# Value products of two pairs of heads in four column groups in the full attention of a twelve-sublayer decoder kernel

## The reference

```python
Q, K, V = (proj(q, w_q), proj(k, w_k), proj(v, w_v))
scores = jnp.einsum('bhqd,bhkd->bhqk', Q, K) / jnp.sqrt(jnp.float32(D_K))
scores = jnp.where(keep, scores, NEG)
attn = jax.nn.softmax(scores, axis=-1)
x = jnp.einsum('bhqk,bhkd->bhqd', attn, V)
```

## Time and profile before

| | us |
|---|---|
| median of 3 runs | 6051.25 (6049.73 to 6057.02) |
| profiled execution | 6049.55 |
| its span in the profile | 6047.7 |
| TensorE busy | 4477.5 (74%) |
| VectorE busy | 3497.5 (58%) |
| ScalarE busy | 2671.6 (44%) |
| GpSimd busy | 1226.0 (20%) |

### The profile page before, as it was taken

One profiled execution on the slowest core, in us unless ns is written; L12 is line 12 of the kernel. 1 busy time (PEld: TensorE's weight loads), 2 busy tenths in 40 slices (PEclk: granted clock), 3 DMA queues, 4 the chain that ended last, 5 costly groups with the idle time before them and its releaser, 6 DMA issues. The chain is left out here.

```text
span 6047.7 us, 135121 instructions
## 1 busy us (share of the span) xinstructions
PE 4477.5 (74%) x46116; PEld 2489.3 (41%) x46246; DVE 3497.5 (58%) x6462; ACT 2671.6 (44%) x5422; POOL 1226.0 (20%) x2792
## 2 busy tenths in 40 slices
PE   1010658686765989768588854799999999999997
PEld 0010232233232222134233322277677767777674
DVE  7998442453434757633433344277777777767775
ACT  0110541353543657545111112366666666666664
POOL 0000110110110101111000000344444444444442
PEclk6555879797877989879699976799999999999998
DMA  1000000000000000000000000000000000000000
GB/s 30 0 0 1 3 5 18 3 1 3 1 23 10 1 1 1 1 11 1 22 23 23 23 10 4 14 31 5 25 5 9 21 6 24 5 25 5 25 6 10
DMA packets 46790, 66.36 MB, mean 11 GB/s; under 512 B 8628, under 2 KB 40480, under 8 KB 44977
## 3 DMA queue, kind: packets, MB, share of 16 engines
q1 hardware_dynamic: 45564, 58.16, 3.2%
q0 software_dynamic: 784, 1.80, 0.2%
HBM read 53.22 MB, written 1.05 MB: 9 GB/s over the span
## 5 line engine op out<-in xcount | busy, mean ns | idle before, releaser
L657 DVE TENSOR_REDUCE minus_max<-banks 128x1 f32<-128x512 f32 (+4 forms) x1152 | 608.3, 569 | 307.9 <-PE banks L551 299.2
L621 ACT ACTIVATE probs<-banks 128x512 f32<-128x512 f32 (+4 forms) x1152 | 580.7, 554 | 347.6 <-PE banks L589 342.4
L2626 POOL TENSOR_TENSOR loc_cos_part<-loc_cos_part,loc_sin_part 128x512 f32<-128x512 f32 x388 | 494.1, 1273 | 698.1 <-DVE loc_sin_part L3055 697.9
L602 PE MATMUL banks<-probs,pair_rows 128*32 128x512 f32 (+3 forms) x2304 | 565.0, 573 | 0.2 <-ACT probs L621 0.2
L2699 PE MATMUL banks<-loc_w_qkv,loc_shifted 128*128 (+1 forms) x1552 | 390.0, 394 | 45.8 <-issue 30.1
L1311 DVE TENSOR_TENSOR product<-gated,banks 128x512 f32<-128x512 f32 x168 | 115.5, 687 | 491.0 <-ACT gated L1293 491.0
L212 POOL TENSOR_SCALAR fin_shifted<-fin_moments 128x4 f32<-128x4 f32 x48 | 14.2, 296 | 1822.9 <-DVE fin_moments L308 1822.9
L1852 PE MATMUL banks<-identity,srt_c 128*128 128x128 f32 x64 | 12.9, 354 | 493.8 <-DVE srt_c L1980 493.8
L1293 ACT ACTIVATE gated<-banks 128x512 f32<-128x512 f32 x168 | 100.3, 597 | 613.6 <-PE banks L1249 613.6
L2699 PEld LDWEIGHTS banks<-loc_w_qkv,loc_shifted 128*128 128x128 f32 x1552 | 281.4, 191 | 88.1 <-issue 32.7
L3088 DVE TENSOR_TENSOR loc_headsT<-banks,loc_sum_inv 128x512 f32<-128x512 f32 x192 | 132.5, 690 | 298.6 <-ACT loc_sum_inv L2960 287.9
(11 more groups left out here) (506 smaller groups left out, 9824.9 us busy)
## 6 DMA issues: line engine op xcount, KB each, us to landing
expert_w<-in_L_ffn_pairs_dram SPq DMA_DIRECT2D x84, 192.0 KB, 2.3
loc_w_qkv<-in_L_ffn_Wqkv_dram SPq DMA_DIRECT2D x7, 1536.0 KB, 8.4
q_stack<-max_rows SPq DMA_DIRECT2D x384, 3.0 KB
loc_v_edge<-loc_v SPq DMA_DIRECT2D x192, 32.0 KB, 1.8
fixed_w<-in_L_ffn_experts_dram SPq DMA_DIRECT2D x8, 514.5 KB, 3.6
loc_pack<-in_L_ffn_pack_dram SPq DMA_DIRECT2D x6, 537.5 KB, 3.6
loc_w_o<-in_L_ffn_Wo_dram SPq DMA_DIRECT2D x6, 512.0 KB, 3.5
loc_scales<-in_L_ffn_scales_dram SPq DMA_DIRECT2D x7, 256.0 KB, 8.4
```

Of the source, the lines that this page charges most:

```text
L602: ins = nc.tensor.matmul(o_bank[at:at + COLS, q0:S], pair_rows[u][:, k, e, :], probs[(a * C + k) % RING][e][:, q0:S], start=(k == 0), stop ...
L621: nc.scalar.activation(probs[(a * C + k) % RING][e][0:kn, q0:S], t_bank[e][0:kn, q0:S], ACT.Exp, scale=scale).then_inc(s["exp_done"], 1)
L657: nc.vector.tensor_reduce(minus_max[:, u, e, qs[0]:qs[0] + len(qs)], view, AX.X, ALU.max, negate=True).then_inc(s["max_done"], 1)
L2626: nc.gpsimd.tensor_tensor(cos_part[:, tiles, :], cos_part[:, tiles, :], sin_part[:, tiles, :], ALU.add).then_inc(s["summed"], 1)
```

## The change

In `attend`:

- The value products of both pairs of a quad are issued together, for each key step four heads in the four column groups of `o_bank`. They are issued in the odd slot for k >= LAG and in the following even slot for k < LAG; the other steps have none. LAG is 2 for C = 4 and 1 for C = 2.
- `probs` has 2 * C couples, one for each step of each pair of a quad: 8 for C = 4, 4 as before for C = 2.
- `act_heads` copies all 128 partitions once per quad, in the even slot, behind `act_rows`.
- Only what is read before it is written is cleared: in context calls the four `k_stack` buffers and the four `probs` buffers of the last, shorter key tile; in self-attention neither. `pair_rows` is cleared as before.
- GpSimd does the maxima of the following pair before the value rows of a pair, in one loop over quads; the rows wait for the values of the quad before.
- An exponential waits for the values of the quad before at its own step.

In the local attention, the head of TensorE's loop is placed at instruction slot 110 of its fetch block.

```diff
@@ -450,7 +450,7 @@
...
     COLS = 32
-    LAG = 2
+    LAG = 2 if n_kt > 2 else 1
     RING = 4
...
@@ -463,7 +463,7 @@
...
         max_rows = sbuf("max_rows", [6, S], BF16)
-        probs = [[sbuf(f"probs{i}_{e}", [P, S]) for e in range(2)] for i in range(RING)]
+        probs = [[sbuf(f"probs{i}_{e}", [P, S]) for e in range(2)] for i in range(2 * C)]
         pair_rows = [sbuf(f"pair_rows{u}", [P, n_kt, 2, COLS]) for u in range(2)]
...
@@ -471,7 +471,8 @@
...
                     "heads_ready", "recip_done", "out_done", "filled", "rows_copied")
-        fills = RING + 2 * RING + 2
+        cleared = [*k_stack, *(buffer for u in range(2) for buffer in probs[u * C + C - 1])] if context else []
+        fills = len(cleared) + 2
         tile_rows = rows[:, :, :].rearrange("p (k h) d -> p k h d", h=H)
...
@@ -501,6 +502,10 @@
...
             return None if isinstance(b, int) and b == B - 1 else (b + 1, a + ahead - PAIRS)
+
+        def quads_of(b, a):
+
+            return b * QUAD + a // 2
 
...
@@ -589,36 +594,36 @@
...
 
-        def pe_values(pe, n, a, k):
-
-            u = a % 2
+        def pe_values(pe, quad, odd, k):
+
             if k == 0:
-                pe.wait_ge(s["rows_copied"], n + 1)
-                pe.wait_ge(s["headsT_copied"], n + 1)
-            pe.wait_ge(s["exp_done"], n * 2 * C + (2 * k + 6))
+                pe.wait_ge(s["rows_copied"], odd + 1)
+                pe.wait_ge(s["headsT_copied"], quad + 1)
+            pe.wait_ge(s["exp_done"], odd * 2 * C + (2 * k + 6))
             q0 = ktiles[k][0] if causal else 0
-            for e in range(2):
-                at = 64 * u + COLS * e
-                ins = nc.tensor.matmul(o_bank[at:at + COLS, q0:S], pair_rows[u][:, k, e, :],
-                                       probs[(a * C + k) % RING][e][:, q0:S],
-                                       start=(k == 0), stop=(k == n_kt - 1), skip_group_check=True)
+            for u in range(2):
+                for e in range(2):
+                    at = 64 * u + COLS * e
+                    ins = nc.tensor.matmul(o_bank[at:at + COLS, q0:S], pair_rows[u][:, k, e, :],
+                                           probs[u * C + k][e][:, q0:S],
+                                           start=(k == 0), stop=(k == n_kt - 1), skip_group_check=True)
             ins.then_inc(s["values_done"], 1)
 
-        def pe_turn_heads(pe, n, rows_before):
-
-            pe.wait_ge(s["headsT_copied"], n + 2)
+        def pe_turn_heads(pe, quads, rows_before):
+
+            pe.wait_ge(s["headsT_copied"], quads + 1)
             pe.wait_ge(s["max_rows_done"], rows_before)
...
 
-        def act_exp(act, n, a, k):
+        def act_exp(act, n, b, a, k):
             k0, kn = ktiles[k]
...
                 act.wait_ge(s["turned_ready"], n * 2 * C + (2 * k + e + 1))
-                act.wait_ge(s["values_done"], n * C + (k + 2))
-                nc.scalar.activation(probs[(a * C + k) % RING][e][0:kn, q0:S], t_bank[e][0:kn, q0:S], ACT.Exp,
+                act.wait_ge(s["values_done"], quads_of(b, a) * C + (k + 1))
+                nc.scalar.activation(probs[(a % 2) * C + k][e][0:kn, q0:S], t_bank[e][0:kn, q0:S], ACT.Exp,
                                      scale=scale).then_inc(s["exp_done"], 1)
...
@@ -634,12 +639,10 @@
...
 
-        def act_heads(act, n, a, quads):
-            u = a % 2
-            act.wait_ge(s["values_done"], n * C + (C + 5))
-            act.wait_ge(s["heads_ready"], quads + 1)
-            half = slice(64 * u, 64 * u + 64)
-            nc.scalar.activation(headsT[half, :], o_bank[half, :], ACT.Copy).then_inc(s["headsT_copied"], 1)
+        def act_heads(act, quad):
+            act.wait_ge(s["values_done"], quad * C + 2 * C)
+            act.wait_ge(s["heads_ready"], quad + 1)
+            nc.scalar.activation(headsT[:, :], o_bank[:, :], ACT.Copy).then_inc(s["headsT_copied"], 1)
 
...
@@ -666,9 +669,9 @@
...
 
-        def pool_rows(pool, b, a, u, n):
-
-            hold(pool, s, s["values_done"], n * C + (5 - C))
+        def pool_rows(pool, b, a, u, quad):
+
+            hold(pool, s, s["values_done"], quad * C + C)
             nc.gpsimd.tensor_copy(pair_rows[u][:, :, :, 0:DH + 1],
...
@@ -702,12 +705,10 @@
...
                 def lagged(n, b, a, k):
-                    if k >= LAG:
-                        pe_values(pe, n, a, k - LAG)
-                    elif isinstance(n, int) and n == 0:
-                        return
-                    else:
-                        pe_values(pe, n - 1, (a - 1) % PAIRS, C - LAG + k)
+                    if a % 2 and k >= LAG:
+                        pe_values(pe, quads_of(b, a), n, k - LAG)
+                    if a % 2 == 0 and k < LAG and not (isinstance(n, int) and n == 0):
+                        pe_values(pe, quads_of(b, a) - 1, n - 1, C - LAG + k)
 
...
@@ -726,10 +727,10 @@
...
                     if a % 2 == 0 and not (isinstance(n, int) and n == 0):
-                        pe_turn_heads(pe, n, n + 2)
+                        pe_turn_heads(pe, quads_of(b, a), n + 2)
 
                 pe.sem_inc(s["max_turned"], 2)
-                pe.sem_inc(s["values_done"], 5)
+                pe.sem_inc(s["values_done"], C)
                 pe.sem_inc(s["heads_ready"], 1)
...
@@ -747,50 +748,48 @@
...
                 for k in range(C - LAG, C):
-                    pe_values(pe, n, PAIRS - 1, k)
+                    pe_values(pe, B * QUAD - 1, n, k)
                 pe.wait_ge(s["out_done"], B * QUAD)
-                pe_turn_heads(pe, n + 1, n + 1)
+                pe_turn_heads(pe, B * QUAD, n + 1)
 
...
                 def slot(n, b, a):
-                    first = isinstance(n, int) and n == 0
-                    act_exp(act, n, a, 0)
+                    closing = a % 2 == 0 and not (isinstance(n, int) and n == 0)
+                    act_exp(act, n, b, a, 0)
                     if C > 2:
-                        act_exp(act, n, a, 1)
+                        act_exp(act, n, b, a, 1)
                     if later(b, a, 1):
                         act_rows(act, n + 1)
+                    if closing:
+                        act_heads(act, quads_of(b, a) - 1)
                     if C > 2:
-                        if not first:
-                            act_heads(act, n - 1, a - 1, quads_of(b, a - 1))
-                        act_exp(act, n, a, 2)
+                        act_exp(act, n, b, a, 2)
                     if later(b, a, 3):
                         act_stack(act, n + 3, (a + 3) % RING)
-                    act_exp(act, n, a, C - 1)
-                    if C == 2 and not first:
-                        act_heads(act, n - 1, a - 1, quads_of(b, a - 1))
-
-                def quads_of(b, a):
-                    return b * QUAD + a // 2
+                    act_exp(act, n, b, a, C - 1)
 
                 act.sem_inc(s["exp_done"], 4)
-                act.sem_inc(s["headsT_copied"], 2)
+                act.sem_inc(s["headsT_copied"], 1)
                 for n in range(3):
...
                 pairs_of(slot, act)
-                n = B * PAIRS - 1
-                act_heads(act, n, PAIRS - 1, n // 2)
+                act_heads(act, B * QUAD - 1)
 
...
                 pool.wait_ge(s["filled"], fills)
-                with pool.Fori(0, B) as b:
-                    with pool.Fori(0, PAIRS // 2) as m:
-                        for u in range(2):
-                            n = b * PAIRS + m * 2 + u
-                            pool_max(pool, u, n)
-                            pool_rows(pool, b, m * 2 + u, u, n)
+                pool_max(pool, 0, 0)
+                with pool.Fori(0, B * QUAD - 1) as quad:
+                    b, a = quad // QUAD, (quad % QUAD) * 2
+                    pool_max(pool, 1, quad * 2 + 1)
+                    pool_rows(pool, b, a, 0, quad)
+                    pool_max(pool, 0, quad * 2 + 2)
+                    pool_rows(pool, b, a + 1, 1, quad)
+                pool_max(pool, 1, B * PAIRS - 1)
+                for u in range(2):
+                    pool_rows(pool, B - 1, PAIRS - 2 + u, u, B * QUAD - 1)
 
...
@@ -807,7 +806,7 @@
...
                 dve.sem_inc(s["out_done"], 1)
-                for buffer in (*k_stack, *(buffer for couple in probs for buffer in couple)):
+                for buffer in cleared:
                     nc.vector.memset(buffer[:, :], 0.0).then_inc(s["filled"], 1)
...
@@ -2898,7 +2897,8 @@
...
                 batch(0, None)
-                with nc.Fori(1, BATCHES, engines=(mybir.EngineType.PE,), hint_back_edge=True) as k:
+                with nc.Fori(1, BATCHES, engines=(mybir.EngineType.PE,), hint_back_edge=True,
+                             head_slot={mybir.EngineType.PE: 110}) as k:
                     batch(k, k - 1)
...
```

## The result

The changed kernel takes 6077.58 us (median of 6 runs, 6073.73 to 6082.19) against 6051.31 for the kernel before: 1.0042 times the time before (95% interval 1.0029 to 1.0055). It is 26 us slower, where 5960 was forecast and 5920 to 6060 was the range. The profiled execution took 6079.52 us, its span 6077.7 (before 6047.7).

What follows compares the result with a forecast made beforehand. TensorE was busiest but did not always set the pace: VectorE's maxima loop did in plain steps, the row transfer in biased context's odd slots. 6049.55 - 119.2 + 30 = 5960 us; range 5920 to 6060.

Steps and rivals of the forecast that it cites:

- The pinned head: TensorE's local loop: no change taken; bounds 30 us less and 30 to 40 us more.
- rival (c): Local loop: the pinned head costs a second fetch at each of 23 turns, +35 us, 5995; chance 0.12.
- The clock in the C = 4 quads: Steps without values: clock falls in one of three of 48 quads, 24 us more, plus 6 for contexts.
- rival (a): Clock falls in every quad: C = 4 alone 72 us, 6002; contexts too 144 us, 6074; chance 0.15.
- fills: Starts of the six attention calls: fewer buffers cleared, 22.6 us less.
- plain quads: Plain self-attention, even slot: the build's step loses its value group, 0.9 us a quad, 28.8 us less over 32.
- causal: Causal quads: no value group before the build, 0.95 us each, 15.2 us less over 16.
- masked: Masked context quads: value group and wait go in even slots, odd gain too; 1.6 us each, 25.6 less over 16.
- biased context: Biased context quads: even slots 5.05 instead of 5.65 us, odd gain 0.15 at most; 0.75 each, 24 less over 32.
- the ends: Ends of the six calls: one heads' copy and, in context, one value group less, 0.5 us each, 3 less.
- (b): Value groups: four column groups run as two after two, freeing TensorE after 1.83 us, not 0.98; 6087; chance 0.10.
- (d): Attention calls: other work fills each gap and only fills and ends stay, 6024 us; chance 0.08.

Runs made afterwards that it cites:

- holder: Changed kernel, loop head at slot 100, plus three matmuls into the query bank in each of odd-slot steps 0 and 1, C = 4: 5923.36 us, 0.9791.
- holder_all: holder plus three such matmuls behind the turned heads at the end of even slots in the three context calls: 5916.43 us, 0.9774 of the kernel before.

## Why the prediction was wrong

- **The pinned head** is the step that failed most. I set it at nothing because "the row itself is the nearest", with bounds of 30 less and 30 to 40 more. The 1.37 us a turn in the earlier trace rows was not a fixed price of a turn; it depends on where the branch lies, and from 0.5 to 3.5 us were measured. Even rival (c) had only the wait (50 us measured, 35 said) and not what a wait of over 3 us does to the clock behind it. I had the means to see that: the earlier trace rows shows a clock that falls when TensorE does little. The term was 89 us, more than twice its upper bound. The sign that I named for (c), turns longer by over 1 us, is there.
- **The clock in the C = 4 quads** was seen, but the number of falls was wrong. I took one fall in three of the 48 quads, 16, at 1.5 us each, and 6 for the contexts, 30 in all. Measured: the clock fell in 40 of 48. By the same kernel with and without the work in the stretch, these falls cost 55 us (`holder` still has 5), 64 with the contexts (`holder_all`, read from one trace each). The price was near: 55 us for 35 falls fewer is 1.6 each, an estimate that counts the added matmuls as free. In the middle of a plain call, the first quads of a sequence aside, a quad with a fall is 1.5 to 2.8 longer than the 15.7 of one without; there the value group alone costs 0.87 (1.87 to the next instruction for 1.00) and the build 1.27 (2.67 for 1.40). In the causal call the added work gains 1.1 a quad. So rival (a), every quad at 1.5 (72 for C = 4), described this part better than the forecast, and its sign, direct products of 0.61 in odd slots, is there. My argument against it, that turned heads, rows and builds fill the stretch, did not hold; in odd slots each of the two steps has only 0.39 + 0.39 us of matmuls, and 0.39 more for the rows.
- **The rest of the sum came out near, in part by luck.** With the clock mostly held the calls take 1391.7 us, 124 less than before, where the terms without the clock add up to 119. One by one, measured (forecast): fills 26.3 (22.6); plain quads 15.82 for 17.03 to 17.07, 1.2 each (0.9); causal 16.37 for 17.28, 0.9 (0.95); masked 10.79 for 12.63, 1.8 (1.6); biased context 9.87 and 9.83 for 10.78 and 10.81, 0.9 to 1.0 (0.75). Four of the five were too small, and the ends had the wrong sign and made up for some of it: 0.5 less each was forecast; from the last scores on they are 0.3 to 1.7 longer in the changed kernel (first context 5.91 for 4.32), 6 us in all. In that call both value groups of the last quad now stand behind the last scores, and their 16 records take 3.42 us (from 814.11) at a granted clock of 0.50. Before, the last 12 records took 2.02 (from 825.78) at 1.00.
- **The even plain slot** fell to 7.26, not to 8.05, and the odd one with a held clock is 8.55, not 8.05. The quad's gain is larger than the one I summed, and its place is another: with no value group ahead of them, the odd slot's first scores start at 2057.66, while its direct product starts only at 2058.39, behind the maxima, so the border between the slots moved forward.
- **Context quads** went nearly as described (biased: even 5.16 and odd 4.60, for the 5.05 and 4.90 of the sum). In the changed kernel, an even slot of the first context call has no wait ahead of the turned heads, and TensorE's idle time now stands at the slot's end, where it waits for the transfer:

```profile
728.22 0.59 ACT L640 ACTIVATE max_rows<-banks 6x512 bf16<-6x512 f32 x1 [0.35 <-PE banks L568]
...
728.71 0.57 ACT L645 ACTIVATE headsT<-banks 128x512 f32<-128x512 f32 x1
...
729.61 0.66 PE L617 MATMUL banks<-identity,headsT 128*128 128x128 f32 x4
...
731.42 0.39 PE L594 MATMUL banks<-q_stack,k_stack 64*128 64x512 bf16 x2 [1.16 <-DMA q_stack<-max_rows]
```

  From the end of the rows' copy (728.22 + 0.59) to 731.42 is 2.61, the 2.62 of before: rows and transfer bound the slot.
- **Rivals (b) and (d)** did not occur: the group of four takes 1.00, and the slots moved. What came is (a) and (c) together, each larger than the forecast's share for it.

## What to carry over

Packing matmuls into column groups takes work away from TensorE, and where VectorE or a transfer sets the pace, the emptied steps can lower its clock for the work that follows; look for the places where all the packed work is gone at once, and price them at both rates, first thing. Where the body of a hardware loop is long (here 2967 instructions, twelve packets of them a turn), treat the place of its head as a parameter to be measured, not as neutral: here five places gave loops from 2037 to 2132 us. And where a wait grows, add what runs at 1.2 GHz behind it: here the clock fell behind 20 of 22 waits of 3.4 to 4.0 us, and behind none of 22 of 1.2 to 1.8.

## What the runs showed of the hardware

Four float32 products of 128 x 32 by 512 in the four column groups take as long as two: 1.00 us to the next instruction against 0.98. The head of a loop of 2967 recorded instructions cost from 0.5 to 3.5 us a turn by its place alone, and its packet of instructions began about 3 us ahead of the turn's first matmul wherever it was placed. And adding 96 x 3 matmuls to a kernel made it 55 us faster in the trace, since TensorE's clock then fell in 5 quads instead of 40; the same matmuls in busy steps made it 42 us slower. The Trainium skill says that activity releases the throttle ("TensorE: Matmul & The Clock Gate", Part 1); the pair of experiments agrees with it.
